# Output bias added on GpSimd while the rows are copied; one DMA per expert for the pad rows; products whose result nothing reads; other banks for the token features

## The chip, the cores and the metric

The kernel runs on one core of a Trainium2 chip. The metric is the device time of one execution in microseconds (us), as the median of several runs. The profile shows one execution of its own: its span goes from the first to the last instruction.

The engines are TensorE (PE; its weight loads are shown as PEld), VectorE (DVE), ScalarE (ACT), GpSimd (POOL) and SyncE (SP), which here issues most DMAs. A q behind a name is that engine's sequencer.

## The reference, cut to what matters

A state space kernel makes 16 x 256 token rows of width 512 from `x`; a class token is put in front. Then come a gated linear recurrence over time with an output product and a skip product, and a mixture of experts (8 experts, 2 for each token, and a shared one):

```python
h = _L0_tok_ref(x, log_dt, B_ri, inv_A_real, A_imag, 512)      # (16, 256, 512)
h = concatenate([broadcast_to(cls_tok, ...), h], axis=1)
...
gates = einsum('btd,de->bte', u, W_in) + b_in      # u: layernorm of layernorm(h)
h_t = (1.0 - a_t) * h_{t-1} + a_t * b_t;  y_t = h_t * tanh(c_t)
out = einsum('bts,sd->btd', y, W_out) + b_out
out = out + einsum('btd,de->bte', x, W_skip) + b_skip
h = h + out
...
h = h + routed(layernorm(h)) + shared(layernorm(h))
```

The change touches where `b_out + b_skip` is added.

## The kernel before, in words

**First stage (lines 293 to 551).** Weights are loaded by SP in 13 jobs, cut into a high and a low f16 half by ScalarE (`st_hi`) and VectorE (`low_half`). VectorE builds tables of powers of the state space poles. At its end it makes `brow` (lines 545 to 547), the sum of the two output biases as two f16 halves in partitions 0 and 32; `ones_row` is a stationary operand of ones.

**Token rounds (`body(k, q)` of every engine, k = -1 to 17; NCH = 16, LAST = 17).** `iterate` (line 705) unrolls k = -1 to 3, loops over ten, and unrolls the rest. A tile number n holds 16 time steps of 16 sequences, 256 rows in two tiles of 128; n = 0 is the class token alone. What this document calls round k is `body(k)`. In it TensorE does, in this order:

- `gate_up_shared(0..3)` of tile k - 1 (line 1018; all its products are L997 of the helper `split3`), with banks `BH` = 1, 2, 0 in turn, then `ranks` (L1043 to L1047);
- `project(0)` of tile k (line 1049): the skip product (L997 with 512 columns) into bank `BS`, the output product (L1059 to L1061) and the bias product `ones_row` x `brow` (L1062) into `BY`;
- `gate_up_shared(4, 5)`, `project(1)`, and `shared_down(0, 1)` (L1072 to L1076) into banks `BD` = 3, 0;
- `input_project` of tile k + 1 (L997), `features` for the tokens of tile k + 2 (line 1001, 64 f32 products, L1011, into `BU` = banks 1 and 2), and the router's products (L997 with 8 columns).

ScalarE copies the features out of `BU` (`tok_out`, L1202), and `gate_up_shared(0)` of the next round waits for that. SP stores them to `h_tok` (L876) and loads them back as rows `hx` in the next round (L819). VectorE takes their statistics (`stats2`, L1521), GpSimd the power -1/2 (L927, L928), ScalarE normalizes (`normalized`, L1222 and L1227) and later copies `hx` to `hc` (L1272), so that `hx` can be loaded again (`c_prom`). VectorE evicts `project` into `h2` (`project_out`: L1540 adds `hc` to the skip product, L1541 adds the output product), evicts `shared_down` (`down_out`, L1553), and makes the operands of `features` (`tok_p`: L1351, L1356; `tok_e`: L1331, L1338, L1339). Nearly all of VectorE's instructions wait for the one before (`link`). GpSimd also scatters the normalized rows to the experts' slots in DRAM, `x_slots` (L941), and computes inv3 and off3 (L950, L951).

In each round SP also loads one unit of expert weights (`load_unit`); ScalarE and VectorE cut it into halves, and SP stores it to `w_halves` (`store_unit`). The first eight units are brought to `wexp` by one DMA that ScalarE issues (line 1300), the other eight by SP during the expert stage, one at every second slot (line 897).

**Pad rows.** Between the experts' rows in `x_slots` unused rows must hold zeros and a row number to which their result is added. `pad_rows(eng, e)` (line 775), called in round NCH by SP for e = 0 to 5 and by ScalarE for 6 and 7, issues two DMAs per expert: 384 pieces of 64 bytes from `pads` (L779) and 384 of 2048 bytes of zeros from `zrow` (L781). Four of SP's six stand ahead of the transposes of `x3w` into `x3T` (L858), which the router's products wait for.

**Expert stage.** 71 slots of 128 rows: TensorE does `gate_up` (L1146, L1147) and, two slots behind, `down` (L1156); the results are added to `out` by an indirect DMA of GpSimd (L975).

The order of work on each engine is the order of its `body`; there is no planner.

## Time and profile before

| | us |
|---|---|
| runs | 1201.67, 1191.70, 1199.46 |
| median | 1199.46 |
| profiled execution, its own time | 1196.48 |
| its span | 1194.8 |
| PE busy | 1059.5 |
| DVE busy | 812.2 |
| POOL busy | 383.9 |
| ACT busy | 347.2 |

The mean granted TensorE clock is 0.944 of full speed. Busy time adds up the instructions; matmuls are pipelined, so that PE's busy time says little of how near it is to its peak. The first stage takes the first 60 us, the token rounds last until about 773 us, and the expert stage takes the rest.

### The profile page before, as it was taken

How to read it: one execution, taken by the hardware profiler on the slowest of the kernel's cores; microseconds unless marked ns; L12 is line 12 of the kernel's file. 1: busy time of each engine (PE TensorE's matmuls, PEld its weight loads, DVE VectorE, ACT ScalarE, POOL GpSimd, SP SyncE). 2: the span in 40 equal slices, each digit the busy share in tenths (PEclk: the TensorE clock that was granted, in tenths of full speed). 3: DMA queues.
4: the chain of work that ended last, by engine and by line, in shares of the span. 5: the costliest groups of instructions: out<-in, count | busy, mean ns of one | idle time of the engine just before them, and what ended most of it. 6: DMA issues, size and time to landing. Idle time of an engine off the chain costs nothing.

```text
span 1194.8 us, 26490 instructions
## 1 busy us (share of the span) xinstructions
PE 1059.5 (89%) x7869; PEld 696.9 (58%) x7870; DVE 812.2 (68%) x2123; ACT 347.2 (29%) x658; POOL 383.9 (32%) x352
## 2 busy tenths in 40 slices
PE   3046898999999999999999994989999999999995
PEld 3034566666766676667766771655555555555552
DVE  7976988898889888988898563544444444444442
ACT  4413433443344333443344332111111111111110
POOL 1011221222123211332022210145545656655554
PEclk8556998999999999999999997899999999999998
DMA  7322456455545555455535589689998777877885
GB/s 247 112 53 54 105 159 154 124 152 173 149 127 150 170 151 143 139 171 162 165 112 157 170 258 371 188 170 217 224 172 132 130 130 130 134 132 128 133 124 74
DMA packets 311150, 183.57 MB, mean 154 GB/s; under 512 B 261218, under 2 KB 280034, under 8 KB 309044
## 3 DMA queue, kind: packets, MB, share of 16 engines
q1 hardware_dynamic: 292948, 135.83, 46.8%
q0 software_dynamic: 15504, 36.46, 15.2%
q10 hardware_dynamic: 2640, 10.54, 2.3%
q8 instruction: 32, 0.52, 0.2%
q14 instruction: 26, 0.21, 0.1%
HBM read 53.40 MB, written 79.73 MB: 111 GB/s over the span
## 4 chain that ended last, share of the span: by engine, by line
PE 75%; DVE 3%; SPq 3%; DMA 3%; issue 2%; ACT 1%; POOLq 0%; POOL 0%; ACTq 0%; DVEq 0%
PE bank L997 30%; PE bank L1146 10%; PE bank L1156 10%; PE bank L1147 10%; PE bank L1072 8%; PE bank L1011 4%; DMA out<-x2w,rows_in 2%; SPq L779 1%; SPq L781 1%; PE bank L1076 1%; ACT tokens L1202 1%; PE bank L1062 1%; DMA wexp<-w_halves 1%; PE bank L1075 1%; DVE wexp L1351 0%
## 5 line engine op out<-in xcount | busy, mean ns | idle before, releaser
L997 PE MATMUL bank<-wexp 128*128 128x256 f16 (+2 forms) x3252 | 418.6, 291 | 24.8 <-issue 9.5
L997 PEld LDWEIGHTS bank<-wexp 128*128 128x128 f16 x3252 | 316.4, 101 | 110.7 <-issue 33.7
L1146 PE MATMUL bank<-wexp,rows_in 128*128 x852 | 255.5, 313 | 9.6 <-issue 6.9
L1147 PE MATMUL bank<-wexp,rows_in 128*128 x852 | 255.1, 312 | 0.0
L975 POOL DMA_INDIRECT out<-x2w,rows_in x71 | 113.7, 1601 | 116.0 <-DMA out<-x2w,rows_in 82.8
L927 POOL TENSOR_TENSOR inv<-var,power 128x4 f32<-128x4 f32 x17 | 29.2, 1717 | 375.0 <-DVE var L1533 375.0
L1689 DVE SCALAR_TENSOR_TENSOR mixed<-bank,mixed 128x352 f32<-128x352 f32 x71 | 37.2, 525 | 161.0 <-ACT mixed L1308 108.4
L963 POOL TENSOR_TENSOR ex<-base,ld 128x8 f32<-128x8 f32 x71 | 120.7, 1699 | 75.9 <-DVE ld L1668 56.0
L1146 PEld LDWEIGHTS bank<-wexp,rows_in 128*128 128x128 f16 x852 | 83.1, 98 | 66.6 <-issue 25.9
L1308 ACT ACTIVATE mixed<-bank 128x352 f32<-128x352 f32 x71 | 32.9, 464 | 295.3 <-PE bank L1147 295.3
L1156 PE MATMUL bank<-wexp,gates 128*128 (+1 forms) x477 | 111.7, 379 | 2.9 <-DVE x2w L1684 2.9
L1072 PE MATMUL bank<-wexp 128*128 128x512 f16 x495 | 112.6, 380 | 0.0
L1147 PEld LDWEIGHTS bank<-wexp,rows_in 128*128 128x128 f16 x852 | 83.2, 98 | 44.2
L1011 PE MATMUL bank<-wexp 64*128 64x64 f32 x1024 | 63.9, 283 | 46.8 <-DVE wexp L1356 46.8
L941 POOL DMA_INDIRECT x_slots<-x3w,sl x66 | 69.8, 1057 | 85.1 <-DVE sl L1413 67.9
L1209 ACT ACTIVATE sgs<-bank 128x256 f32<-128x256 f32 (+1 forms) x102 | 38.4, 376 | 199.5 <-PE bank L997 197.6
L1011 PEld LDWEIGHTS bank<-wexp 64*128 64x128 f32 x1024 | 61.7, 197 | 50.4 <-issue 49.3
L1072 PEld LDWEIGHTS bank<-wexp 128*128 128x128 f16 x495 | 45.8, 98 | 57.9 <-issue 7.2
L1351 DVE TENSOR_TENSOR wexp<-wexp 128x1024 f32 (+1 forms) x64 | 77.8, 1221 | 0.8 <-issue 0.2
L1156 PEld LDWEIGHTS bank<-wexp,gates 128*128 128x128 f16 (+1 forms) x477 | 46.6, 98 | 53.0 <-issue 4.2
L1374 DVE SCALAR_TENSOR_TENSOR gf<-bank,sgs 128x256 f32<-128x256 f32 (+1 forms) x102 | 42.5, 416 | 45.6 <-ACT sgs L1209 38.7
L1691 DVE TENSOR_TENSOR mixed<-mixed 128x352 f16<-128x352 f32 x71 | 37.3, 525 | 41.8 <-ACT mixed L1312 40.1
(281 smaller groups left out, 1247.3 us busy)
## 6 DMA issues: line engine op xcount, KB each, us to landing
w_halves<-rows_in SPq DMA_DIRECT2D x16, 704.0 KB
wexp<-w_halves ACTq DMA_DIRECT2D x1, 8704.0 KB
wexp<-w_halves SPq DMA_DIRECT2D x8, 1088.0 KB
h_tok<-tokens SPq DMA_DIRECT2D x16, 512.0 KB, 2.7
mixed<-h_tok SPq DMA_DIRECT2D x32, 256.0 KB
out<-h SPq DMA_DIRECT2D x32, 256.0 KB
w_halves<-rows_in SPq DMA_DIRECT2D x16, 384.0 KB
rows_in<-in_L_ffn_w_gate SPq DMA_DIRECT2D x16, 352.0 KB, 5.4
```

The source lines that it names most:

```text
L941: nc.gpsimd.indirect_dma_start(out=xs_d.bitcast(I32), out_offset=bass.IndirectOffsetOnAxis(ap=sl[:, i, c:c + 1], axis=0), in_=x3w[:, i, :] ...
L963: nc.gpsimd.tensor_tensor(ex[:, b % 2, 0, :], base[:], ld[:, b % 2, :], ALU.pow).then_inc(d_ex, 1)
L975: nc.gpsimd.indirect_dma_start(out=out_rows, out_offset=bass.IndirectOffsetOnAxis(ap=ext[b][:, E:E + 1].bitcast(I32), axis=0), in_=yo[b % ...
L997: last = MM(dst, stat_of(step, a), mov_of(step, b), start=(s_ == 0 and a + b == 0), stop=(s_ == len(steps) - 1 and a == 1))
L1011: last = MM(BU[t][:, j * NA:(j + 1) * NA], pp[q, f, j].rearrange("p b c -> p (b c)"), ea[q, f, j, :], start=(f == 0), stop=(f == 1))
L1072: MM(BD[i][:], gT[:, m, a, t], wsd[:, m, b, :], start=(m == 0 and a + b == 0), stop=False)
L1146: MM(GB[:, 0:H], xT[b][:, a, c, :], wexp[:, u, o:o + H], start=s_, stop=e_)
L1147: last = MM(UB[:, 0:H], xT[b][:, a, c, :], wexp[:, u, o + H:o + 2 * H], start=s_, stop=e_)
L1156: last = MM(DB[:], gT2[b % 4][0:HK[c], a, c, :], wexp[0:HK[c], bass.ds(unit, 2), o:o + D // 2], start=(c == 0 and a + w == 0), stop=(c == ...
L1209: A(sgs[P - p1:P, m % 2, 0:w], BH[m % 3][0:p1, 0:w], ACT.Silu, scale=SXW).then_inc(c_sg, 1)
L1351: ch.do(TT((pp, pt)[f % 2][:, f // 2], cc, hh, ALU.mult))
L1374: STT(gf[p0:P, m % 2, 0:w], u, SXW, sgs[p0:P, m % 2, 0:w], ALU.mult, ALU.mult).then_inc(c_gm, 1)
```

## The change

1. **Bias.** `bias` [128, 512] f32 and `bsk` are loaded with both biases broadcast to all partitions and added on VectorE at the end of the first stage; `brow`, `ones_row` and L1062 go (33 products). The copy of `hx` to `hc` goes from ScalarE to GpSimd, at the end of its `body`, as an addition of `bias`.
2. **Pad rows.** `pads` in DRAM holds whole rows of 2112 bytes. Its zeros are written in round 1 by four DMAs of SP, its numbers in round 2. `pad_rows` is one DMA. SP's call for e = 4 stands between the two transposes of `x3w`.
3. **Banks.** `BU` = `BD` (banks 3 and 0). `features` waits for `c_dev` in place of `c_gm`; the wait for `c_toke` stands at m = 2 of `gate_up_shared` in place of m = 0.
4. **Products whose result nothing reads.** 36 before `features` of round -1, 10 after a wait for `c_toke` and 28 ahead of `input_project` in round 0, all into `BD[0]`.
5. **Expert weights.** The DMA of line 1300 stands at the head of ScalarE's `body(15)` in place of its end. The other eight units are loaded at every third slot from slot 1, and SP's part of the expert stage is unrolled for 24 slots in place of 16.

```diff
-                sp.dma_start(bo[:, 0, :], b_out.rearrange("(a n) -> a n", a=1)).then_inc(p_in, 16)
-                sp.dma_start(bo[:, 1, :], b_skip.rearrange("(a n) -> a n", a=1)).then_inc(p_in, 16)
+                sp.dma_start(bias[:], b_out.rearrange("(a n) -> a n", a=1).broadcast_to([P, D])).then_inc(p_in, 16)
+                sp.dma_start(bsk[:], b_skip.rearrange("(a n) -> a n", a=1).broadcast_to([P, D])).then_inc(p_in, 16)
...
-                ch.do(nc.vector.memset(brow[:], 0.0))
...
-                link(TT(bo[:, 2, :], bo[:, 0, :], bo[:, 1, :], ALU.add))
-                link(TS(brow[0:1, :], bo[:, 2, :], SW * SY, None, ALU.mult))
-                link(STT(brow[32:33, :], bo[:, 2, :], SW * SY, brow[0:1, :], ALU.mult, ALU.subtract))
+                link(TT(bias[:], bias[:], bsk[:], ALU.add))
...
-        BU = [psum[1], psum[2]]
         BH = [psum[1], psum[2], psum[0]]
         BD = [psum[3], psum[0]]
+        BU = BD
...
-            eng.dma_start(xs_d[bass.ds(row, 3 * P), 2 * D:XW].bitcast(I32),
-                          pads_d[e].rearrange("r q w -> (r q) w")[bass.ds(turn, 3 * P)]).then_inc(c_z, 16)
-            eng.dma_start(xs_d[bass.ds(row, 3 * P), 0:2 * D].bitcast(I32).rearrange("(i p) w -> p i w", p=P),
-                          zrow[:, 0:2 * D].bitcast(I32).rearrange("p (o w) -> p o w", o=1).broadcast_to([P, 3, D])).then_inc(c_z, 16)
+            eng.dma_start(xs_d[bass.ds(row, 3 * P), :], pads_d[e].rearrange("r q w -> (r q) w")[bass.ds(turn, 3 * P), :]).then_inc(c_z, 16)
...
                         for i in range(tiles(n)):
+                            if i == 1 and isinstance(k, int) and k == NCH:
+                                pad_rows(sp, 4)
                             sp.wait_ge(c_lo3, n * 2 + (i + 1) * 2 // tiles(n))
...
                     if isinstance(k, int) and k == NCH:
-                        for e in range(4, 6):
-                            pad_rows(sp, e)
+                        pad_rows(sp, 5)
...
+                    if isinstance(k, int) and k == 1:
+                        for r in range(4):
+                            sp.dma_start(pads_d[:, r, :, 0:2 * D].bitcast(I32).rearrange("e q w -> q e w"),
+                                         zrow[:, 0:2 * D].bitcast(I32).rearrange("p (o w) -> p o w", o=1).broadcast_to([P, E, D])).then_inc(c_pw, 16)
...
-                    if isinstance(i, int) and i < 2 * E and i % 2:
-                        u = E + i // 2
+                    if isinstance(i, int) and i < 3 * E and i % 3 == 1:
+                        u = E + i // 3
                         sp.dma_start(wexp[:, u, :], w16_d[u]).then_inc(d_w, 16)
...
+                    if has(k + 1):
+                        n, nt = k + 1, tiles(k + 1)
+                        gp.wait_ge(c_hx, (n + 1) * 32)
+                        at_least(gp, c_oev, n * 2)
+                        apart(gp, c_sep)
+                        TT(hc[:, 0:nt, :], hx[:, 0:nt, :], bias[:].rearrange("p (o d) -> p o d", o=1).broadcast_to([P, nt, D]),
+                           ALU.add).then_inc(c_prom, 1)
...
                     if not isinstance(k, int) or k >= 1:
-                        pe.wait_ge(c_gm, k * 6)
+                        pe.wait_ge(c_dev, k * 2)
...
+                        if m == 2:
                             at_least(pe, c_toke, clampc(k + 1) * 2)
-                        if m == 2:
                             at_least(pe, c_dev, n * 2)
...
-                        MM(BY[:], yT[:, 1, t], wout[:, 0, :], start=False, stop=False)
-                        MM(BY[:], ones_row[:], brow[:], start=False, stop=True).then_inc(c_out, 2 // tiles(n))
+                        MM(BY[:], yT[:, 1, t], wout[:, 0, :], start=False, stop=True).then_inc(c_out, 2 // tiles(n))
...
+                    def idle_products(count):
+
+                        for i in range(count):
+                            MM(BD[0][:], ident16[:], wskip[:, 0, 0, :], start=True, stop=True)
+
                     if isinstance(k, int) and k == -1:
+                        idle_products(36)
                         features(k)
+                    if isinstance(k, int) and k == 0:
+                        pe.wait_ge(c_toke, 2)
+                        idle_products(10)
...
+                    if isinstance(k, int) and k == 0:
+                        idle_products(28)
                     if first_win:
                         input_project()
...
                 def body(k, q):
+                    if isinstance(k, int) and k == NCH - 1:
+
+
+                        act.wait_ge(c_tokm, NCH * 2)
+                        act.wait_ge(c_wo, 32 * E)
+                        act.dma_start(wexp[:, 0:E, :], w16_d[0:E].rearrange("u p n -> p u n")).then_inc(d_w, 16)
...
-                    if has(k + 1):
-                        n, nt = k + 1, tiles(k + 1)
-                        at_least(act, c_oev, n * 2)
-                        A(hc[:, 0:nt, :], hx[:, 0:nt, :], ACT.Copy).then_inc(c_prom, 1)
```

The waits on `c_pw`, `c_z` and `p_gp` follow the new counts.

## Rows read from the trace of the kernel before

**Rows 1.** The page's chain that ended last, shares of the span by engine

```profile
PE 75%; DVE 3%; SPq 3%; DMA 3%; issue 2%; ACT 1%; POOLq 0%; POOL 0%; ACTq 0%; DVEq 0%
```

**Rows 2.** Windows, two rounds: length, busy us per engine, PEclk, DMA share, GB/s

```profile
391.01:431.32 40.31, 39.75 (x327) 27.73 (x328) 34.38 (x79) 15.17 (x29) 9.01 (x11) 0.96 0.49 146
431.32:470.01 38.69, 38.13 (x328) 26.91 (x328) 34.34 (x79) 15.28 (x29) 8.98 (x11) 1.00 0.51 152
```

**Rows 3.** PE timeline, round from 431.32: start, length, line, operation [idle before <-releaser]

```profile
452.55 0.38 PE L1061 MATMUL bank<-wexp,yT 128*128 128x512 f16 x1
453.18 3.41 PE L1072 MATMUL bank<-wexp 128*128 128x512 f16 x15
464.97 3.79 PE L1011 MATMUL bank<-wexp 64*128 64x64 f32 x64
470.01 5.19 PE L997 MATMUL bank<-wexp 128*128 128x256 f16 x46 [0.56 <-ACT tokens L1202]
```

**Rows 4.** DVE timeline of the same round

```profile
437.19 0.42 DVE L1374 SCALAR_TENSOR_TENSOR gf<-bank,sgs 128x256 f32<-128x256 f32 x1 [1.21 <-ACT sgs L1209]
439.91 0.42 DVE L1374 SCALAR_TENSOR_TENSOR gf<-bank,sgs 128x256 f32<-128x256 f32 x1 [0.22 <-ACT sgs L1209]
462.11 0.68 DVE L1553 SCALAR_TENSOR_TENSOR h<-bank,h 128x512 f32<-128x512 f32 x1
468.83 0.69 DVE L1338 TENSOR_TENSOR wexp<-wexp 128x512 f32<-128x512 f32 x1 [0.89 <-PE bank L1011]
```

**Rows 5.** POOL timeline: first stage, round -1, and the round from 431.32

```profile
1.40 0.99 POOL L324 MEMSET zrow<- 128x1056 f16 x1
68.38 1.24 POOL L928 TENSOR_TENSOR off<-neg,inv 128x2 f32<-128x2 f32 x1 [0.18 <-POOL inv L927]
458.04 0.60 POOL L951 TENSOR_TENSOR off<-neg,inv 128x1 f32<-128x1 f32 x1 [0.18 <-POOL inv L950]
```

**Rows 6.** Line L1351, all its instructions: ns min/median/max, first and last start

```profile
L1351 DVE TENSOR_TENSOR wexp<-wexp x64: 1215/1219/1227, 66.1 to 650.7; 128x1024 f32 x40, 128x1024 f32<-128x1024 f32 x24
```

**Rows 7.** DVE timeline, end of the first stage

```profile
52.72 0.68 DVE L545 TENSOR_TENSOR bo<-bo 1x512 f32<-1x512 f32 x1
```

**Rows 8.** PE timeline, rounds -1 and 0

```profile
73.25 7.09 PE L1011 MATMUL bank<-wexp 64*128 64x64 f32 x64 [46.15 <-DVE wexp L1356]
103.50 6.10 PE L997 MATMUL bank<-wexp 128*128 128x256 f16 x36 [8.75 <-issue]
```

**Rows 9.** SP and DVE timelines, rounds 1 and 2

```profile
148.10 0.38 SPq L876 DMA_DIRECT2D h_tok<-tokens  x1
158.84 1.28 DVE L1521 BATCH_NORM_STATS2 stat<-mixed 128x6 f32<-128x512 f32 x2
```

**Rows 10.** DMA issues of the first 30 us: queue, KB, us to landing

```profile
x_slots<-zrow SPq DMA_DIRECT2D x1, 1792.0 KB, 13.4
x_slots<-zt SPq DMA_DIRECT2D x1, 56.0 KB, 12.8
```

**Rows 11.** Window in round 16: the same columns as rows 2

```profile
718.00:722.00 4.00, 4.00 (x19) 1.62 (x18) 1.78 (x4) 1.14 (x3) 0.00 (x0) 1.00 1.02 424
```

**Rows 12.** ACT, SP and PE timelines, round 16

```profile
699.19 0.44 ACTq L1300 DMA_DIRECT2D wexp<-w_halves  x1
717.73 8.72 SPq L779 DMA_DIRECT2D x_slots<-pads  x1
748.47 0.48 PE L997 MATMUL bank<-gw,wexp 128*128 128x8 f16 x12 [19.27 <-DMA wexp<-x3w]
```

**Rows 13.** DMA issues: all 16 of one form, then its one after 700 us

```profile
rows_in<-in_L_ffn_w_down SPq DMA_DIRECT2D x16, 256.0 KB, 4.6
rows_in<-in_L_ffn_w_down SPq DMA_DIRECT2D x1, 256.0 KB, 28.6
```

**Rows 14.** Windows in the expert stage: the same columns as rows 2

```profile
829.00:884.00 55.00, 51.30 (x301) 29.02 (x300) 23.47 (x81) 8.64 (x18) 28.75 (x18) 1.00 1.19 211
884.00:928.00 44.00, 43.81 (x260) 25.22 (x259) 20.60 (x72) 7.68 (x16) 26.10 (x16) 1.00 0.80 132
```

More of the change, by code:

```diff
@@ L210, in vit_tower @@
             bin_ = t0("bin_", [P, 3], F32)
-            bo = t0("bo", [1, 3, D], F32)
+            bsk = t0("bsk", [P, D], F32)
             st = [t0(f"st{i}", [P, 4, D], F32) for i in range(2)]
@@ L324, in _ @@
                 nc.gpsimd.memset(zrow[:], 0.0).then_inc(p_gp, 1)
-                nc.gpsimd.memset(ones_row[:], 1.0).then_inc(p_gp, 1)
-                gp.wait_ge(p_gp, 6)
+                gp.wait_ge(p_gp, 5)
                 for m in (ident16, identf):
@@ L381, in _ @@
             def _(pe):
-                pe.wait_ge(p_gp, 8)
+                pe.wait_ge(p_gp, 7)
                 def turn(g):
@@ L828, in body @@
                         sp.wait_ge(c_ri, 1)
-                        sp.wait_ge(c_pw, 64)
+                        sp.wait_ge(c_pw, 128)
                         for e in range(4):
@@ L900, in _ @@
                 sp.wait_ge(d_w, 16)
-                over_tiles(sp, serve, 2)
+                over_tiles(sp, serve, 3)
                 for b in range(2):
@@ L936, in body @@
                         if isinstance(k, int) and k == LAST:
[L937 removed]
+                            gp.wait_ge(c_z, 16 * E)
                         apart(gp, c_sep)
@@ L1254, in body @@
                         act.wait_ge(c_ri, 1)
-                        act.wait_ge(c_pw, 64)
+                        act.wait_ge(c_pw, 128)
                         pad_rows(act, 6)
@@ L1294, in body @@
                         gate_tanh()
-                    if isinstance(k, int) and k == NCH - 1:
-                        act.wait_ge(c_tokm, NCH * 2)
-                        act.wait_ge(c_wo, 32 * E)
-                        act.dma_start(wexp[:, 0:E, :], w16_d[0:E].rearrange("u p n -> p u n")).then_inc(d_w, 16)
                 act.wait_ge(c_cst, 2)
```

14 lines of the change are left out of this document (6 added, 8 removed).

## The prediction

> **What bounds the kernel now.** I read the chain that ended last first: TensorE has 75% of it, no other engine over 3% [rows 1]. So a product taken away counts where TensorE is not waiting, and a wait counts where TensorE is what waits. Then I cut the span into rounds by the start of L997 after the router's products. From round 3 to 14 a round takes 38.7 us, or 40.3 us where the granted clock dipped (mean 0.96 in place of 1.00): four of these twelve rounds have that dip, at 1.62 us each [rows 2]. TensorE is busy 98% of such a round, with one hole, the 0.56 us at the start where L997 waits for ScalarE's copy of the token features [rows 3]. VectorE is busy 34.4 of the 38.7 us [rows 2], and its instructions are linked one to the next, so that its real idle time in the round is only 1.21 + 0.22 + 0.89 = 2.3 us, in three waits [rows 4]. That is the second bound, and the one to keep in mind: a round cannot go under about 36.4 us for VectorE, whatever TensorE saves.
>
> **Rounds 3 to 14, TensorE's side.** Between the start of the third L1061-type product and the first product of L1072 lie 0.63 us, the deleted L1062 in between; 15 products of L1072 have a pace of (3.41 - 0.38) / 14 = 0.22 us [rows 3]. Without L1062 the gap is one pace: 0.41 us saved, twice a round, 0.82 us. The new banks move the wait for the features' copy to the third group (m = 2), over 5 us later, when the copy is long done: the 0.56 us go too. TensorE's round becomes 38.69 - 1.38 = 37.31 us. The price of the banks is a new wait of `features` for both `down_out`s: the second starts at 462.11 and takes 0.68 us, `features` starts at 464.97 [rows 3, 4]. Of 2.2 us slack, 0.8 go with the products, so it still costs nothing while VectorE keeps its times. Queued behind it are the router's products and the whole next round.
>
> **The same rounds, the copy of the rows.** ScalarE loses a copy it had time for (busy 15.3 of 38.7 us [rows 2]): nothing. GpSimd gets an addition of 128x1024 f32 with two SBUF inputs after its last L951, from about 458.8 [rows 5]. No row has such an operation. From below: VectorE does that shape in 1.22 us [rows 6]. From above: a memset of 1056 columns took GpSimd 0.99 us [rows 5]; two reads and a write at that pace are 2.9 us. Its own lateness costs nothing, since SP asks for it in the next round, ten us on. What may cost is the way to SBUF: L928 on two columns took 1.24 us at 68.38 while VectorE ran four L1351 back to back, against 0.2 to 0.3 elsewhere [rows 5], so GpSimd waits until a VectorE instruction of two SBUF inputs is over. The reverse is not seen: 64 L1351 took 1.215 to 1.227 us, beside GpSimd's short operations or not [rows 6]. A long one may hold VectorE's L1356, which is due at 459.24, by 0 to 2.6 us. I take 1.3 us, near the lower end because the only rows are those in which VectorE is not held. What VectorE can do, 36.4 us a round, then becomes 36.4 + 1.3 = 37.7 us, more than TensorE's 37.31: `features` waits 0.4 us for the second `down_out`, and the round is VectorE's. The gain is 1.0 us a round, 12 rounds: **-12 us**. Without any hold it is 12 x 1.38 = -16.5.
>
> The Trainium skill speaks against this edit: "SBUF — State Buffer", section "Who interferes with whom", says that VectorE with two SBUF inputs and GpSimd reading SBUF exclude each other, the first to issue keeping the shared ports for its whole instruction. By "GPSIMD Engine Reference", section 3.1, an addition of 2048 elements takes 4.5 us there, so some 2.3 us as an estimate here. The 1.24 us of L928 agree with the rule for one direction; the other direction no row shows.
>
> **First stage and first rounds.** At the end of the first stage VectorE is last: three operations (0.68 [rows 7], 0.42, 0.68) give way to one of 0.68. The biases now arrive as 256 KB each in place of 2 KB, and the first activation waits for all nine small loads: I give back 0.7 us. **-0.5 us**. The 36 idle products run while TensorE waits 46 us for VectorE. `features(-1)` took 7.09 us with the clock at its lower level (1.2 GHz), 3.79 us in a round at 1.00, which is 2.4 GHz [rows 3, 8]: 3.3 us, all on the path, since ScalarE's copy, the store and the load of the next rows follow it. The 10 and the 28 cover the wait for yT and the 8.75 us before L997 at 103.50, whose 36 products took 6.10 us [rows 8] and need 4.1 at the 5.19 us for 46 of rows 3; they are ended before their data come. Perhaps 2.2 us of the other cold products return. **-5.5 us**.
>
> **The zero rows in round 1.** Four new DMAs on SP write 4 x 2 MB = 8.4 MB in 2 KB pieces right behind the store at 148.10 [rows 9]. Behind them on the same queue stand the rows hx of tile 3, the weight unit's loads and stores, and the transposes. Is a queue served in order? The 56 KB of zt, issued 1.3 us behind 1792 KB of zeros, landed after 12.8 us [rows 10]: yes. The most that the engines moved is 424 GB/s [rows 11]; 8.4 MB are 20 us. So hx lands at about 148.5 + 1.5 + 20 + 3.5 = 173.5 in the times of before; `stats2` takes it at 158.84 [rows 9]. Behind `stats2` on VectorE stand `project_out` and all else, and rounds 1 and 2 are the ones that VectorE bounds: **+14.5 us**. Add GpSimd's hold in those two rounds, **+2.6 us**.
>
> **The load of wexp one round earlier.** ScalarE issued it at 699.19 [rows 12]; at the head of the body it comes at about 663.6. Before, it filled the DMA engines from 702 to 746 us and the pad rows had to be issued through them: one issue alone held SP for 8.72 us, and x3T came so late that TensorE stood 19.27 us [rows 12]. With the load gone from there, one DMA of whole rows for two per expert, and only pad row 4 between the transposes, I expect x3T of tile 1 12.5 us after its `project`, as in other rounds, plus 2 us of pad traffic: a hole of some 6.5 us, 13 gained. But round 15 now meets the load. The small loads issued beside it landed after 28.6 us, where 4.6 is the median of their 16 [rows 13]: two queues get turns by packets, not by bytes. hx of tile 16 is 2048 packets of 256 B, 128 for each engine; the load is 64 packets of 8.7 KB for each. It will land with the end of the load, some 27 us into the round, where `stats2` wants it at 10.5; TensorE has 4 us slack there: +12.2. Together **-0.8 us**. In rounds 15 and 16, where VectorE has little to do, the products give 2 x 0.82 + 0.56 = **-2.2 us**.
>
> **Expert stage.** Between 829 and 884 us TensorE lost 3.7 of 55 us with the DMA share at 1.19; with no loads of weight units left the share was 0.80 and the loss 0.2 of 44 [rows 14]. Every third slot in place of every second thins the loads by a third, over a longer stretch. Of some 5 us lost to them in all, **-3 us**.
>
> **Sum.** -12 - 0.5 - 5.5 + 14.5 + 2.6 - 0.8 - 2.2 - 3 = -6.9. From the profiled execution (1196.5 us; its span is 1194.8) that is 1189.6, say **1190 us**; the median of the three runs, 1199.5, lies 3 us above the profiled one, which is inside their spread of 10 us.
>
> **Rivals.** *GpSimd's addition holds VectorE fully* (0.25). By the port rule above it starts while VectorE is in `down_out`, gets the ports, and holds L1356 to its end: 2.0 to 2.6 us. Then VectorE's `down_out` is what `features` waits for, and the round is 38.4 to 39.0 us. The point from which it decides is a hold of 0.9 us; from 2.3 us on a round is longer than the 38.69 of before. At 2.6: +3.7 in place of -12, and 2.6 more in rounds 1 and 2: **1208 us**, slower. For it: L928. Against: 64 unchanged L1351. *The zero rows are hidden* (0.25): the engines serve hx beside them, or hx is early enough: without 14.5, **1175 us**; with hx of tile 16 on time as well, 1163. For it: DMA stands idle half of rounds 1 and 2. Against: the order that zt shows. *The clock decides, not the products* (0.10): the stretch of `features` and the router is where the clock fell in 4 of 12 rounds; a change of where the waits lie can give it to all twelve (+13, **1203 us**) or to none (-6.5, 1183). Then the change doesn't do what it says in those rounds.
>
> **Chances.** The forecast has 0.40, with a range of its own of 1182 to 1199. For eight in ten I reach down to 1168 and up to 1209. About 1% can be told from no change here. Faster by more (below 1187.5): the hidden rows, a third of the forecast, half of the clock's case: 0.44. Slower by more (above 1211.5): 0.15. Within: 0.41.
>
> **What would show it.** In the profile after: rounds of 37.3 to 38 us from 3 to 14 with no ScalarE wait at their start; if a hold, L1356 late or longer beside a GpSimd addition of 2 us, and `features` waiting for L1553. In round 2 a wait of `stats2` for hx of about 14 us, and one of some 16 us in round 15; a hole under 8 us in place of 19.27. If both waits for hx are missing I am wrong by 25 us. If the addition takes over 4 us, the round is VectorE's or GpSimd's and the sum falls on the other side.

## The result: slower by 1.4%, and the profile after

The changed kernel took 1212.0 us (median of four runs, 1210.4 to 1214.0) where the kernel before, run beside it, took 1195.6 (1191.2 to 1201.7): a ratio of 1.0138, 95% interval 1.010 to 1.018. Forecast were 1190 us and a range of 1168 to 1209. The profiled execution took 1213.5 us (span 1211.8), 17.0 us over that of before.

The page's chain that ended last, after, against [rows 1]:

```profile
PE 39%; DVE 29%; issue 10%; DMA 6%; SPq 2%; ACT 1%; DVEq 1%; POOL 0%; POOLq 0%; ACTq 0%
```

VectorE has 29% of the chain where it had 3%: the rounds changed hands. To see where the 17 us are I cut both spans at one instruction: the second eviction of `shared_down` in each round (L1553 before, L1562 after; round 1 has one).

| stretch | before | after | difference | forecast |
|---|---|---|---|---|
| first stage | 60.3 | 62.6 | +2.3 | -0.5 |
| to the end of round 1 | 79.8 | 79.6 | -0.1 | -4.2 |
| rounds 2 and 3 | 84.8 | 110.2 | +25.4 | +14.8 |
| rounds 4 to 14 | 430.5 | 421.1 | -9.4 | -11.0 |
| rounds 15 to 17 | 118.1 | 118.5 | +0.4 | -3.0 |
| expert stage | 421.2 | 419.7 | -1.6 | -3.0 |

The first stage is taken to end at VectorE's first instruction of the rounds (L1654 before, L1663 after). The last column is my sum, spread over the same stretches (the 2.6 us of hold half to round 1, half to round 2). Its 23.9 us of error have no one place.

**A steady round.** Windows of two rounds after; columns as in [rows 2]:

```profile
442.90:480.79 37.89, 37.19 (x327) 26.84 (x325) 35.76 (x80) 14.22 (x28) 11.30 (x12) 1.00 0.53 156
480.79:518.98 38.19, 37.38 (x327) 26.92 (x325) 35.78 (x80) 14.22 (x28) 11.45 (x12) 1.00 0.52 154
```

VectorE is busy 35.8 us where it was 34.3 [rows 2]. The 1.4 us more are in one instruction. Timelines of VectorE, GpSimd and TensorE around the end of a round after, and the line L1365 (L1356 before) as a whole:

```profile
475.71 0.69 DVE L1562 SCALAR_TENSOR_TENSOR h<-bank,h 128x512 f32<-128x512 f32 x1
476.32 3.94 DVE L1365 TENSOR_TENSOR wexp<-wexp 128x1024 f32<-128x1024 f32 x2
480.19 0.68 DVE L1486 SCALAR_TENSOR_TENSOR x3w<-wexp,x3w 128x512 f16<-128x512 f32 x1
480.79 0.68 DVE L1562 SCALAR_TENSOR_TENSOR h<-bank,h 128x512 f32<-128x512 f32 x1
```

```profile
475.68 2.37 POOL L954 TENSOR_TENSOR mixed<-mixed,bias 128x1024 f32<-128x1024 f32 x1
```

```profile
443.73 3.79 PE L1015 MATMUL bank<-wexp 64*128 64x64 f32 x64 [0.70 <-DVE h L1562]
```

```profile
L1365 DVE TENSOR_TENSOR wexp<-wexp x32: 1209/1221/2810, 73.0 to 671.9; 128x1024 f32<-128x1024 f32 x32
```

GpSimd starts its addition 0.03 us ahead of a VectorE instruction that reads PSUM and one SBUF operand, and that one keeps its 0.69 us. The next, with two SBUF operands, starts at 476.32 and takes 2.8 us in place of 1.2: it ends 1.1 us after GpSimd does (478.05), which is about its own length. Two of them took 3.94 us, where they took 2.35 before. So the hold is 1.5 to 1.6 us, and `features` waits 0.70 us for the second `down_out`. By the Trainium skill ("SBUF — State Buffer", section "Who interferes with whom") the first to issue keeps the shared ports for its whole instruction; this is the direction that no row of before showed, and the trace agrees.

**First stage and first rounds.** ScalarE's first activation, which VectorE's chain waits for, and TensorE's timeline in rounds -1 and 1:

```profile
9.67 0.20 ACT L347 ACTIVATE pw_<-dtj 128x2 f32<-128x2 f32 x1 [7.55 <-DMA bsk<-in_L_attn_b_skip]
```

```profile
63.24 9.35 PE L1085 MATMUL bank<-wexp,ident 128*128 128x512 f16 x36 [34.43 <-DVE m L1666]
76.38 7.09 PE L1015 MATMUL bank<-wexp 64*128 64x64 f32 x64 [3.79 <-DVE wexp L1365]
...
146.78 5.97 PE L1015 MATMUL bank<-wexp 64*128 64x64 f32 x64 [2.52 <-DVE wexp L1365]
```

Windows of round -1 after, columns as in [rows 2]:

```profile
66.13:76.37 10.24, 6.46 (x30) 2.74 (x28) 9.95 (x15) 1.44 (x2) 5.29 (x3) 1.00 0.01 2
76.37:86.61 10.24, 10.23 (x95) 10.12 (x96) 4.49 (x9) 1.09 (x2) 0.00 (x0) 0.50 0.25 73
```

Before, that activation started at 6.23 us: the two broadcast loads make it 3.4 us late, of which 2.3 are left at the end of the stage. The 36 idle products ended 3.8 us ahead of `features(-1)`, which took 7.09 us, exactly as in [rows 8]. They did raise the granted clock, to 1.00 from 66.1 us on; it fell back to 0.50 at 76.37, just as `features(-1)` started after those 3.8 idle us. In round 1 `features` had waited 0.7 us and run at 2.4 GHz before; now it waits 2.5 us and takes 5.97 in place of 3.79.

**Rounds 2, 15 and 16.** SP's queue behind the store of round 1, then VectorE in round 2:

```profile
153.96 0.38 SPq L869 DMA_DIRECT2D h_tok<-tokens  x1
154.37 12.45 SPq L872 DMA_DIRECT2D pads<-zrow  x4
166.94 10.84 SPq L811 DMA_DIRECT2D mixed<-h_tok  x2
```

```profile
182.44 1.29 DVE L1530 BATCH_NORM_STATS2 stat<-mixed 128x6 f32<-128x512 f32 x2 [17.79 <-DMA mixed<-h_tok]
```

The zeros went at 377 GB/s (window 166 to 170), and `stats2` got its `hx` 28.5 us after the store was issued. In round 15, VectorE, TensorE, and the DMA issues from 666 to 730 us:

```profile
707.76 1.29 DVE L1530 BATCH_NORM_STATS2 stat<-mixed 128x6 f32<-128x512 f32 x2 [17.09 <-DMA mixed<-h_tok]
```

```profile
712.92 5.29 PE L1001 MATMUL bank<-wexp 128*128 128x512 f16 x12 [13.21 <-DVE h L1550]
763.59 0.48 PE L1001 MATMUL bank<-gw,wexp 128*128 128x8 f16 x12 [3.79 <-DMA wexp<-x3w]
766.73 0.48 PE L1001 MATMUL bank<-gw,wexp 128*128 128x8 f16 x12 [2.65 <-DMA wexp<-x3w]
```

```profile
wexp<-w_halves ACTq DMA_DIRECT2D x1, 8704.0 KB, 27.3
...
h_tok<-tokens SPq DMA_DIRECT2D x1, 512.0 KB, 10.4
```

All as forecast: the store beside the load of `wexp` lands after 10.4 us (median of all: 2.7), `stats2` waits 17.1 us, TensorE 13.2, and the hole of 19.27 [rows 12] is 6.4 us in two parts.

### The profile page after: what moved, and what is told of

It reads as the page before. It is cut to its first block, busy times and chain, and to the rows that moved or that the text cites. A ratio compares the mean times of both kernels' runs of the same rounds, so it can differ in the third digit from the quotient of the medians.

```text
span 1211.8 us, 26540 instructions
## 1 busy us (share of the span) xinstructions
PE 1068.8 (88%) x7910; PEld 706.1 (58%) x7911; DVE 834.4 (69%) x2120; ACT 330.2 (27%) x641; POOL 421.4 (35%) x368
## 4 chain that ended last, share of the span: by engine, by line
PE 39%; DVE 29%; issue 10%; DMA 6%; SPq 2%; ACT 1%; DVEq 1%; POOL 0%; POOLq 0%; ACTq 0%
PE bank L1160 10%; PE bank L1170 10%; PE bank L1161 10%; PE bank L1001 5%; DVE wexp L1360 3%; DMA mixed<-h_tok 2%; DVE wexp L1340 2%; DVE wexp L1376 2%; DVE h L1549 2%; DVE h L1550 2%; DVE stat L1552 2%; DVE x3w L1486 2%; DVE wexp L1365 1%; DVE stat L1530 1%; PE bank L1015 1%
## 5 line engine op out<-in xcount | busy, mean ns | idle before, releaser
L1001 PE MATMUL bank<-wexp 128*128 128x256 f16 (+2 forms) x3252 | 419.5, 291 | 42.9 <-DVE h L1550 31.7
L1001 PEld LDWEIGHTS bank<-wexp 128*128 128x128 f16 x3252 | 316.3, 101 | 130.7 <-DVE h L1550 32.4
L1170 PE MATMUL bank<-wexp,gates 128*128 (+1 forms) x477 | 111.7, 379 | 2.6 <-DVE x2w L1693 2.6
L1015 PE MATMUL bank<-wexp 64*128 64x64 f32 x1024 | 67.8, 293 | 16.2 <-DVE h L1562 9.7
L1360 DVE TENSOR_TENSOR wexp<-wexp 128x1024 f32 (+1 forms) x64 | 77.8, 1221 | 1.4 <-issue 1.0
L1015 PEld LDWEIGHTS bank<-wexp 64*128 64x128 f32 x1024 | 65.8, 207 | 20.4 <-issue 13.3
```

The costliest lines, as they stand in the source:

```text
L1001: last = MM(dst, stat_of(step, a), mov_of(step, b), start=(s_ == 0 and a + b == 0), stop=(s_ == len(steps) - 1 and a == 1))
L1015: last = MM(BU[t][:, j * NA:(j + 1) * NA], pp[q, f, j].rearrange("p b c -> p (b c)"), ea[q, f, j, :], start=(f == 0), stop=(f == 1))
L1170: last = MM(DB[:], gT2[b % 4][0:HK[c], a, c, :], wexp[0:HK[c], bass.ds(unit, 2), o:o + D // 2], start=(c == 0 and a + w == 0), stop=(c == ...
L1360: ch.do(TT((pp, pt)[f % 2][:, f // 2], cc, hh, ALU.mult))
```

## The experiments

Each ran beside the kernel before. First the stretches of the table above, in us, from the one profile that each kernel has (rounds 4 to 14 hold up to three dips of the clock, 0.6 to 2.9 us each, and in e7 and e9 one of 4.2):

| kernel | first stage | to end of 1 | 2, 3 | 4 to 14 | 15 to 17 | expert | ratio to before |
|---|---|---|---|---|---|---|---|
| changed | 62.6 | 79.6 | 110.2 | 421.1 | 118.5 | 419.7 | 1.0138 |
| e1 zeros in the first stage | 65.3 | 77.9 | 93.8 | 421.5 | 117.7 | 419.7 | 1.0062 |
| e2 bias on TensorE | 60.5 | 76.2 | 103.2 | 419.0 | 122.7 | 420.4 | 1.0034 |
| e3 addition in the gap | 63.8 | 77.8 | 106.2 | 409.9 | 119.8 | 420.2 | 1.0036 |
| e4 load at the end | 63.7 | 79.7 | 111.4 | 423.8 | 118.3 | 419.2 | 1.0128 |
| e5 before, bias alone | 63.8 | 79.3 | 93.0 | 420.4 | 112.7 | 418.8 | 0.9982 |
| e6 load in mid-round | 64.6 | 79.4 | 108.9 | 423.7 | 118.6 | 419.7 | 1.0197 |
| e7 zeros spread | 63.3 | 79.8 | 91.6 | 423.0 | 119.1 | 418.7 | 1.0037 |
| e8 no idle products | 63.9 | 78.1 | 111.3 | 423.7 | 118.7 | 418.8 | 1.0173 |
| e9 pads undone | 63.4 | 79.8 | 91.6 | 428.5 | 116.5 | 424.2 | 1.0040 |
| e10 load in pieces | 63.4 | 79.6 | 110.2 | 424.7 | 114.7 | 419.5 | 1.0167 |
| e11 four repairs | 59.4 | 75.9 | 88.5 | 409.9 | 123.6 | 417.9 | 0.9824 |
| e12 the same, bias on TensorE | 60.5 | 76.2 | 85.6 | 418.9 | 113.6 | 418.1 | 0.9879 |
| e13 e5 with products | 63.4 | 80.5 | 88.9 | 419.5 | 114.1 | 417.9 | 0.9922 |
| e14 pieces on SP | 63.6 | 78.2 | 111.2 | 421.3 | 111.7 | 419.7 | 1.0103 |
| e15 e11, pieces on SP | 59.1 | 76.7 | 89.0 | 411.7 | 111.1 | 422.5 | 0.9762 |
| e16 e15 with products | 59.5 | 76.2 | 88.0 | 409.9 | 108.2 | 423.1 | 0.9741 |

The intervals of the ratios are 0.0025 to 0.008 wide to each side; those that matter stand in the text. A stretch of a single profile has a scatter of its own: with the load of `wexp` at the same place, rounds 15 to 17 take 116.5 to 122.7 us (changed, e1, e2, e3, e7, e8, e9).

The dips are not spread evenly. Where TensorE has no wait next to `features` in a steady round (e2, e3, e11, e12, e15, e16), rounds 4 to 14 hold one dip in six profiles; where it waits 0.5 to 0.7 us there (before and all others), every profile has one to three. A whole stretch of e3, rounds 4 to 14, columns as in [rows 2]:

```profile
247.80:657.70 409.90, 409.25 (x3578) 295.23 (x3575) 383.60 (x860) 157.43 (x308) 126.07 (x132) 1.00 0.54 159
```

That the wait brings the dips is how I read it; no run adds the wait alone.

### The zeros (e1, e7, e9)

e1 and e7 move the same four DMAs, e9 undoes part 2 (no zeros in `pads`, `pad_rows` as two DMAs):

In e1 they stand behind the weight loads 6, 8 and 12 of the first stage, in e7 behind `load_unit` of rounds 0 to 2 and ahead of the transposes:

```diff
-                    if isinstance(k, int) and k == 1:
-                        for r in range(4):
...
+                    for r in {6: (0, 1), 8: (2,), 12: (3,)}.get(i, ()):
...
```

```diff
+                    if isinstance(k, int) and 0 <= k < 3:
+                        for r in ((0, 1), (2,), (3,))[k]:
...
```

> The changed kernel with one thing moved: the four DMAs that write the zeros of the pad rows (8.4 MB) are issued by SP in the first stage, between its weight loads, in place of round 1. Theory (a queue is served in order, so the rows hx stood behind the zeros): the wait of stats2 for hx in round 2 (17.8 us) goes, rounds 2 and 3 take what they took before, and the time falls by 19 to 24 us, from 1212 to 1188 to 1193. Rival 1 (the zeros cost as much wherever they are, through the DMA engines): the weight loads of the first stage are late in turn, the first stage ends 5 us or more later than its 63, and the time falls by 12 or less. Rival 2 (something else than hx is late in round 2): it falls by under 5.

Measured: 1201.7 us, 10 less than the changed kernel, not 19 to 24. The wait of `stats2` is gone and rounds 2 and 3 fall by 16.4 us to 93.8, but not to the 84.8 of before; the first stage takes 65.3. So rival 1 holds in part (the first stage is 2.7 us longer, not 5), and 9 us of rounds 2 and 3 are not the zeros'.

> The changed kernel with the four DMAs of zeros issued where SP's queue has nothing due for ten us: two in round 0, one each in rounds 1 and 2, each behind the loads of hx and of the weight unit and ahead of the transposes of x2w. Theory (only the order on the queue costs): round 2 falls from 67.0 us to 49, as with the zeros in the first stage, and the first stage keeps its 62.6 to 63.7 us (with the zeros in it: 65.3): 1190 to 1195. Rival (8.4 MB delay whatever moves beside them in the DMA engines too): the transposes of rounds 0 to 2 are late, each round 2 to 5 us longer, 1200 to 1205.

Measured: 1199.1 us (ratio 1.0003 to 1.0071), 4 over the range expected, rounds 2 and 3 at 91.6, round 2 at 47.5, the first stage at 63.3. Rounds 2 and 3 fall by 18.6 us, the median of the runs by 12.9; the profile has 1.9 us of the difference in rounds 4 to 14, in a longer dip, and the ten runs spread over 14 us. 8.4 MB moved beside rounds 0 to 2 cost nothing that can be seen where the queue had time; in rounds 2 and 3 the order on the queue was the whole cost, 18.6 us.

> The changed kernel with part 2 (the pad rows) undone: no zeros written in round 1, two DMAs for each expert in round 16 as before, in the order of before. Theory: round 2 is 49 to 50 us in place of 67.0 (as in the run with the bias alone, 49.6), the first stage stays at 62.6 to 63.8 us; rounds 15 to 17 are 118 us as in the changed kernel, since what costs there is the load of wexp: 1194 to 1198, 17 us under the changed kernel. Rival (the single DMA for each expert gains something in round 16, as its 13 us shorter hole suggests): rounds 15 to 17 take 123 to 130 us, 1200 to 1207.

Measured: 1201.2 us. Rounds 2 and 3 take 91.6 as with the zeros spread, though here no zeros are written at all: a second witness. Rounds 15 to 17 take 116.5, so the two DMAs for each expert were no loss there. The total is 3 us over the range expected: in the profile the expert stage took 424.2, for a reason that I did not find, and rounds 4 to 14 took 428.5 with three dips.

### The bias (e2, e3, e5, e13)

e2 undoes part 1 in the changed kernel. e3 keeps it and moves two things: GpSimd's addition (`add_bias`) goes ahead of its second power of the round, and VectorE's first `down_out` ahead of `rows_lo(k, 0)` and the fourth `tok_p`:

```diff
                         for i in range(nt):
+                            if i == nt - 1 and has(k + 1):
+                                add_bias(k + 1)
                             gp.wait_ge(c_st3, n * 2 + (i + 1) * 2 // nt)
...
+                    if shared:
+                        down_out(0)
...
```

> The changed kernel with part 1 (the bias) undone: the bias product on TensorE again, the copy of hx to hc on ScalarE, the small loads of before; all else as changed. Theory (GpSimd's addition holds VectorE for 1.5 us of every round and so takes back what TensorE saves): rounds 3 to 14 become TensorE's again at 38.69 - 0.56 = 38.1 us, with the dips of the clock visible in some, +0 to +6 over 12 rounds; the first stage gives back 2.3 and the first rounds some 2 to 3. Together 1207 to 1213: part 1 as made is worth about nothing. Rival (the addition costs nothing that matters, and the slower time is all from the zero rows and the load of wexp): 12 x 0.82 = 10 us more in the rounds against 2 less in the first stage, 1218 to 1222.

Measured: 1202.1 us, better than expected: ratio 1.0034 against 1.0138. Rounds 4 to 14 take 419.0, as with part 1 (421.1 with one dip), which is the theory; 38.09 us each, as the 38.13 worked out for TensorE. But the first stage, rounds -1 to 1 and rounds 2 and 3 gave 2.1 + 3.4 + 7.0 us, where I expected 4 to 5. Rounds 15 to 17 took 4.2 of it back. Part 1 as made was a loss of 10 us, and it arises early. `features(-1)` shows one piece of it:

```profile
73.29 5.45 PE L1013 MATMUL bank<-wexp 64*128 64x64 f32 x64 [2.39 <-DVE wexp L1368]
```

Without the addition beside VectorE's last operand of round -1 (2.17 us in the changed kernel, 1.2 here), `features(-1)` starts 2.4 us after the 36 products in place of 3.8, and takes 5.45 us in place of 7.09.

> The changed kernel, all of its work kept, but GpSimd's addition is issued before its second power of the round, where VectorE runs instructions that read PSUM or one SBUF input, and VectorE does its first down_out before rows_lo(0) and the fourth tok_p. Theory (the addition holds a VectorE instruction with two SBUF inputs for as long as it runs): the long L1365 (2.7 us) is 1.22 again, VectorE's floor is 36.4 to 36.9 us, and a round is TensorE's at 37.3 to 37.5 us: 0.6 us less in 12 rounds, less what dips of the clock give back, 1203 to 1208. Rival (L1365 is long for another reason, as its place beside the end of the round's DMAs): L1365 stays at 2.7, rounds stay at 38.0 to 38.2, 1211 to 1213.

Measured: 1200.3 us, 12 less than the changed kernel and under the range. VectorE at the end of a round, GpSimd, and windows of two rounds of e3:

```profile
466.26 1.25 DVE L1491 SCALAR_TENSOR_TENSOR x3w<-wexp,x3w 128x512 f16<-128x512 f32 x1
467.44 1.21 DVE L1365 TENSOR_TENSOR wexp<-wexp 128x1024 f32 x1
468.68 2.36 DVE L1370 TENSOR_TENSOR wexp<-wexp 128x1024 f32<-128x1024 f32 x2
```

```profile
464.61 2.35 POOL L923 TENSOR_TENSOR mixed<-mixed,bias 128x1024 f32<-128x1024 f32 x1 [3.35 <-DVE h L1555]
```

```profile
434.51:471.56 37.05, 37.05 (x327) 26.75 (x325) 34.83 (x79) 14.33 (x28) 11.46 (x12) 1.00 0.54 159
471.56:509.08 37.52, 37.37 (x328) 26.94 (x327) 34.97 (x80) 14.33 (x28) 11.48 (x12) 1.00 0.53 157
```

The pair of L1370 takes 2.36 us again. The hold has moved with the addition and shrunk: L1491, the only instruction with two SBUF operands that the addition's tail still meets, takes 1.25 in place of 0.68. TensorE has next to no wait in the round, which takes 37.26 us on average (37.31 worked out).

> The kernel before with part 1 of the change alone: the two biases broadcast and added, GpSimd's addition at the end of its body, no bias product, no copy on ScalarE. Theory from the run with part 1 undone (which gained 10 us, all of it ahead of round 4): first stage +2 to +3.5 (VectorE's first dependent instruction waits for the two 256 KB loads), rounds -1 to 3 +7 in VectorE's holds and in the clock that TensorE loses while it waits, rounds 4 to 14 -0.5 each with the dips hidden, -8: within 4 us of before, 1196 to 1202. Rival (the early loss in the run with part 1 undone came from its meeting with the zero rows): -5 or better, 1192 or less.

Measured: 1195.2 us, ratio 0.9982 (0.9953 to 1.0011): no difference from before, just under the range. Rounds 4 to 14 give 10 us (38.04 us a round without dips in place of 38.69, and fewer dips), rounds 2 and 3 take 8.2 back, the first stage 3.5 (rounds 15 to 17 gave 5.4, which I did not look into). So the early loss does not need the zeros. Three holds of 1.5 us make 4.5 of the 8.2. What makes the rest? e13 puts ten products ahead of `features` in rounds 1 and 2:

```diff
+                    if isinstance(k, int) and k in (1, 2):
+                        pe.wait_ge(c_gm, k * 6)
+                        for i in range(10):
+                            MM(psum[1][:], ident16[:], wskip[:, 0, 0, :], start=True, stop=True)
                     pe.wait_ge(c_tokp, n)
```

> The kernel before with part 1 alone (1195.2 us, rounds 2 and 3 together 93.0 us where before has 84.9), and ten products whose result nothing reads ahead of features in rounds 1 and 2, where TensorE waited 2.3 to 2.5 us for VectorE and features then took 5.6 to 7.1 us in place of 3.8. Theory (a hold of 1.5 us on VectorE grew to 8 us over two rounds because TensorE, waiting, fell to its lower clock, and its slower products then kept VectorE waiting): features takes 3.8 us in both, and rounds 2 and 3 take 85 to 89 us, 4 to 8 less. Rival (VectorE's own work sets these rounds, whatever TensorE's clock): 92 to 94 us and the same total.

Measured: 1188.8 us, ratio 0.9922 (0.9892 to 0.9953), rounds 2 and 3 at 88.9. TensorE in rounds 1 and 2, and the windows of rounds 2 and 3, first of e5, then of e13:

```profile
147.61 6.47 PE L1014 MATMUL bank<-wexp 64*128 64x64 f32 x64 [2.47 <-DVE wexp L1354]
...
192.16 6.63 PE L1014 MATMUL bank<-wexp 64*128 64x64 f32 x64 [2.32 <-DVE wexp L1354]
```

```profile
143.07:192.64 49.57, 44.09 (x352) 32.45 (x352) 43.39 (x96) 17.17 (x34) 13.35 (x13) 0.90 0.40 115
192.64:236.07 43.43, 41.83 (x333) 30.49 (x332) 37.53 (x84) 13.38 (x26) 11.19 (x12) 0.84 0.54 143
```

```profile
145.76 2.32 PE L1010 MATMUL bank<-wexp,ident 128*128 128x512 f16 x10
148.44 3.79 PE L1018 MATMUL bank<-wexp 64*128 64x64 f32 x64 [0.36 <-DVE wexp L1358]
...
186.35 2.32 PE L1010 MATMUL bank<-wexp,ident 128*128 128x512 f16 x10
189.04 3.79 PE L1018 MATMUL bank<-wexp 64*128 64x64 f32 x64 [0.37 <-DVE wexp L1358]
```

```profile
143.88:189.51 45.63, 44.16 (x372) 30.90 (x372) 43.25 (x95) 17.08 (x34) 13.37 (x13) 1.00 0.43 125
189.51:232.82 43.31, 39.37 (x333) 27.85 (x332) 37.44 (x83) 13.37 (x26) 11.19 (x12) 0.92 0.53 143
```

With the gap filled the clock stays at 1.00 through round 2, `features` takes 3.79 us both times, and round 2 is 3.9 us shorter with VectorE's work unchanged (43.4 and 43.3 us busy). That is the amplifier: a hold of 1.5 us makes TensorE wait 2.3 to 2.5 us, where it had waited 0.7 in round 1 and not at all in round 2; while `features` runs the granted clock is 0.56 and 0.54 on average, and the slower products then keep VectorE waiting. The medians fell by 6.4 us, of which these two rounds are 4.1. Of the 8.2 us of e5, 4.1 were clock and about 4 the holds themselves. The split is rough: the clock is at its lower level for 23.9 us of rounds 2 and 3 in e5, for 6.8 in e13 and for 10.2 in the kernel before.

### The idle products (e8)

> The changed kernel without the 36, 10 and 28 products whose result nothing reads. Theory (the 36 end 3.8 us before features(-1) starts, and by then the granted clock has fallen again; the 10 and the 28 warm the project of round 0, which nobody waits for long): the time changes by less than 2 us, 1210 to 1214. Rival (they do warm what is on the path): 3 to 6 us slower, 1215 to 1218.

Measured: 1214.4 us, ratio 1.0173 (1.010 to 1.025) against 1.0138 (1.010 to 1.018): no difference that can be told. In its profile `features(-1)` took 7.09 us after 48 us of waiting, as with the 36 products; up to round 1 it is not slower, and the rest are dips (rounds 5 and 7). The products of round 0 do warm what follows them: 12 products of `project` take 2.75 us behind them and 5.25 in e8, but nobody waits for these, since `features(0)` starts at 112.96 and 112.67 us. The same kind of product, placed with no gap ahead of `features`, works (e13), and with a gap of 2.4 us in place of 3.8 the 36 work by half (e2).

### The load of wexp (e4, e6, e10, e14)

One place each: the end of `body(15)` (e4), behind `normalized(16)` (e6), eight DMAs on ScalarE's queue from there on (e10), eight on SP's queue (e14, shown):

```diff
                     if htok(k):
                         load_unit(k - 1)
+                    if isinstance(k, int) and k in (NCH - 1, NCH):
...
+                        for u in range(4):
+                            u += 4 * (k - NCH + 1)
+                            sp.dma_start(wexp[:, u, :], w16_d[u]).then_inc(d_w if u == E - 1 else d_w8, 16)
```

> The changed kernel with one thing undone: ScalarE issues the load of wexp (8.7 MB) at the end of its body(15), as before. Theory (the load makes late what is loaded beside it, wherever it stands): the wait of stats2 in round 15 goes, 13 us, and the wait for x3T in round 16 comes back, but not whole, since the pad rows are now one DMA for each expert: a hole of 12 to 19 us in round 16 where it is about 6, in all 1204 to 1212. Rival (the pad rows' two DMAs, not the load, made the hole of before): the hole stays under 8 us, and the time falls by 12 or more, to 1200 or less.

Measured: 1214.8 us. Rounds 15 to 17 take 37.0, 44.8 and 36.4 us in place of 52.9, 33.3 and 32.2: the wait has moved and the sum, 118.3, has not. The hole ahead of the router in round 16 is 22.1 us in two parts (19.27 before), so the single DMA for each expert does not shorten it. The total is a few us over the expected range; that is in rounds 2 to 14, with a second dip.

> The changed kernel, but ScalarE issues the load of wexp in body(15) behind its normalization of tile 16, when the rows hx of tile 16 have landed, in place of ahead of everything. Theory (only what is loaded beside it is late, so place it where nothing stands that is due soon): stats2 in round 15 waits no longer (-13), the transposes of x2w and x3w in rounds 15 and 16 are what runs beside it, and they cost 3 to 8: 1201 to 1207. Rival (the transposes are due as soon as hx was, and wait as long): 1209 to 1214.

Measured: 1217.9 us; rounds 15 to 17 take 37.5, 47.9, 33.2, again 118.6. The wait of `stats2` is gone, and TensorE waits 15.3 us for a transpose of `x2w` instead: the rival, and worse. The three equal sums are in part luck, beside a scatter of 116.5 to 122.7 us with the load at one place.

> The changed kernel, but the load of wexp (8.7 MB) is issued by ScalarE as eight DMAs of one unit each, spread over body(15) from behind the normalization of tile 16 and the start of body(16). So far the sum of rounds 15 to 17 was 118.1 to 118.6 us with the load at the end of body(15), at its head and in its middle. Theory (it is the burst that makes the transposes and rows beside it late, the engines having half of their time free): the sum falls by 6 to 14 us, 1198 to 1206. Rival (the bytes cost their time wherever and however they are issued): the sum stays within 3 us of 118, 1209 to 1215.

Measured: 1216.5 us, over both ranges, with rounds 15 to 17 at 114.7. Less than hoped, and no firm figure, since the same pieces gave 123.6 us in e11 and 113.6 in e12: ScalarE reaches five of its eight points within 13 us, so this is still a burst.

> The changed kernel with the load of wexp in eight DMAs of one unit on SP's own queue, four in round 15 and four in round 16, each time behind the loads of the weight unit and ahead of the transposes. On one queue they cannot stand beside a transpose, only ahead of it. Theory (the transposes of x2w and x3w, of some thousand small packets, are made late by turns with large packets of another queue: 16 us to land where 3.3 is usual): the sum of rounds 15 to 17, 118 us so far and 114.7 with the pieces on ScalarE's queue, falls to 105 to 110: 1199 to 1205. Rival (the bytes are what costs): 115 to 120, 1209 to 1215.

Measured: 1210.1 us, in the rival's range; rounds 15 to 17 at 111.7, 6.8 under the changed kernel, between theory and rival. On one queue it does help: the three profiles with the pieces on SP's queue (e14, e15, e16) take 108.2 to 111.7 us there, the three with them on ScalarE's (e10, e11, e12) 113.6 to 123.6. DMA issues with their time to land, e11 (pieces on ScalarE's queue, see below) from 645 to 690 us and e14 from 670 to 760:

```profile
wexp<-w_halves ACTq DMA_DIRECT2D x5, 1088.0 KB, 11.2
...
wexp<-x2w SPq DMA_TRANSPOSE x2, 16.0
wexp<-x3w SPq DMA_TRANSPOSE x2, 16.6
```

```profile
x_slots<-pads SPq DMA_DIRECT2D x6, 792.0 KB, 14.2
...
wexp<-x3w SPq DMA_TRANSPOSE x5, 4.6
wexp<-x2w SPq DMA_TRANSPOSE x2, 6.6
```

A transpose beside the pieces lands after 16 us, behind them on the same queue after 4.6 to 6.6 (usual: 3.0 to 3.3). That fits what the Trainium skill says ("DMA: Bandwidth & Descriptors", section "Queues, rings and completion order"): an engine goes round the queues that have work for it by packets. What the profile lists as packets are here 256 bytes long for the transposes and 8704 for the pieces. It agrees; it doesn't exclude that the bytes set a floor as well, and what is left of the holes in e14 stands beside the pad rows, which took 14.2 us to land.

### Versions that beat both kernels (e11, e12, e15, e16)

e11 joins e3, e7, e10 and later bias loads (behind the fifth weight load, with a semaphore of their own). e12 has e7 and e10 with the bias on TensorE. e15 is e11 with the load as in e14, and e16 adds the ten products of e13.

> The changed kernel with four repairs: GpSimd's addition in VectorE's gap, the zeros spread over rounds 0 to 2, the two bias loads issued between the weight loads with a semaphore of their own, the load of wexp in eight pieces. If the terms add up (-12, -13, -2, and -10 if the pieces do what they should): 1212 - 37 = 1175, without the gain of the pieces 1185. If the early rounds keep VectorE as their bound and the terms overlap: 1185 to 1190.

Measured: 1173.8 us, ratio 0.9824 (0.9785 to 0.9862), where the terms add up to 1175, but not by them: rounds 15 to 17 took 123.6 us by the transposes above in place of giving 10, and the first stage (59.4, with the bias loads late) and the rounds up to 1 gave 6.9.

> The changed kernel with the bias back on TensorE (part 1 undone), the zeros spread and the load in pieces: from the run with part 1 undone (1202) -13 for the zeros and -10 for the pieces if they work: 1179, without them 1189. Against the version with GpSimd's addition in the gap it tells what the bias on GpSimd is worth once it no longer holds VectorE: the rounds 4 to 14 are 37.2 us there and 38.1 here, 10 us for that one, if the early rounds cost both the same.

Measured: 1180.5 us (median of five runs; a sixth took 1196.2), ratio 0.9879 (0.9837 to 0.9920). Rounds 4 to 14: 409.9 in e11, 418.9 here; rounds 2 and 3: 88.5 and 85.6. So in these rounds the bias on GpSimd is worth 6 us once it is in VectorE's gap (9.0 late, less 2.9 early). The medians, 6.7 us apart, agree, but the two intervals overlap, and in the two profiles rounds 15 to 17 differ by 10.0 us the other way.

> The version that beat both kernels (1173.8 us) with the pieces on SP's queue as in the run before. There rounds 15 to 17 took 123.6 us, since the transposes landed after 16 us. Theory: 105 to 110 us, so 1156 to 1162. Rival (bytes): 118 to 124, 1168 to 1176.

Measured: 1171.8 us, ratio 0.9762 (0.9720 to 0.9803). Rounds 15 to 17 at 111.1, 12.5 less than e11; but one dip, and an expert stage of 422.5 that I can't explain, take most of it back, and the total lies in the range of the rival.

> The same with the ten products ahead of features in rounds 1 and 2. Rounds 2 and 3 together took 88.5 us in the version that beat both. If the clock is what is lost there: 84 to 86, 3 us less than the run before. If GpSimd's addition in the gap leaves TensorE no long wait there, no change within 1 us.

Measured: 1167.5 us, ratio 0.9741 (0.9705 to 0.9777), the best of all, 44 us under the changed kernel. Rounds 2 and 3 gained 1.0 us, not 3; the rest of the 4 us to e15 lies in rounds where nothing was changed. The ten products are worth little once the hold is short.

## Why the prediction was wrong, step by step

- **Rounds 3 to 14, TensorE's side** (37.31 us): right. It can be read where VectorE doesn't hold it: 37.26 in e3. That the banks alone leave 38.13: 38.09 in e2.
- **The copy of the rows** (addition 2.0 to 2.6 us, hold 1.3, period 37.7): the mechanism was right, the addition took 2.36 us, the hold 1.5 to 1.6, the period 38.06. The 1.3 was the middle of 0 to 2.6, not worked out, so that its closeness is luck, and so is the gain over rounds 4 to 14: of the 9.4 us, near the 11, 6.9 are the period and 2.5 the dips, for which the sum had no term. The periods before hold 4.9 us of dips (430.5 less 11 x 38.69), those after 2.4, in one dip. Part 1 gave nothing in these rounds on top of the banks (e2: 38.09 without it); alone it gives the same 38.04 (e5). The two do not add up: with part 1 in, VectorE and the hold set the round, with the banks or without.
- **"Add GpSimd's hold in those two rounds, +2.6 us"**: this step failed. Part 1 alone costs 8.2 us in rounds 2 and 3 (e5). I priced the hold on VectorE as if TensorE's products kept their length, and only as large as 1.3 us. In a stretch where VectorE is the bound and TensorE waits, the wait costs clock: 4.1 us of the 8.2 (e13). The rest is the holds themselves: three of 1.5 us fall in this stretch, and I had added 1.3 us for it. The rival in which the clock decides looked at rounds 3 to 14, where TensorE hardly waits.
- **The zero rows in round 1** (+14.5): the mechanism was right, the size was not. Spread, they free 18.6 us. At 377 GB/s the 8.4 MB are 22.3 us, not 20 at the 424 of [rows 11]; and TensorE comes back at 1.2 GHz: L1001 at 190.03, after 16.3 us of waiting, took 5.3 us where 2.75 is usual at 2.4 GHz.
- **The idle products** (-5.5): this step failed, and it is the second largest miss. I took the clock of `features(-1)` to rise because TensorE was busy for 9 us before. But `features(-1)` starts 13 us after the first stage [rows 8], and 36 products last 8 us at the 0.22 of [rows 3] (9.4 measured): they ended 3.8 us ahead of it, and it ran at 1.2 GHz all the same. The trace of before had both numbers. Part 1 made the gap wider: without it the gap is 2.4 us and 1.6 of the 3.3 us come (e2).
- **"I give back 0.7 us"** for the 256 KB bias loads: mis-sized. It was 3.4 us at the first activation, 2.3 at the end of the stage. Issued later under their own semaphore they cost nothing (59.4 in e11).
- **The load of wexp** (-0.8 as a gain of 13 and a loss of 12.2): both sides came as worked out, a gain of 13 in rounds 16 and 17 and a loss of 13 in round 15. That it gains nothing at any place was not seen: 118.3, 118.5 and 118.6 us at the end, the head and the middle. **Products of rounds 15 and 16** (-2.2): probably hidden in those waits, which no run shows.
- **Expert stage** (-3): -1.6, inside a scatter of 418 to 424 us between kernels with the same loads and instructions there, which stays open; part 5 there was not run alone.
- **The chances**: the forecast's own range of 1182 to 1199 left no room for four small misses on one side. Of the rivals, the full hold of VectorE, 1208 us, was nearest in time and wrong in cause: the steady rounds did not get longer.

## What to carry to other kernels

Before an operation goes from a busy engine to an idle one, look at which SBUF operands the neighbour reads in that moment; the same 2.4 us of GpSimd cost 1.5 us beside a two-operand VectorE instruction and 0.6 when placed mostly beside instructions that read PSUM. The zeros cost by what stood behind them on their queue, and nothing by their bytes once they stood where nothing was due; the load of `wexp` cost by the small-packet transfers beside it on the other queue. So put a large DMA where its queue has nothing due, and look at what runs beside it. And where TensorE waits, price the wait twice, in time and in clock.

## What the runs showed of the hardware

- A wait of 2.3 to 2.5 us ahead of 64 small products made them take 6.0 to 6.6 us in place of 3.79 (changed, e5); with ten filler products in the gap (wait 0.4 us) they took 3.79 (e13). In round -1, 36 filler products raised the granted clock to 1.00; when they ended 3.8 us early the 64 ran at 0.50 (7.09 us), at 2.4 us early they took 5.45 (e2).
- Rounds 4 to 14 of the six profiles in which TensorE has no wait next to `features` hold one dip of the granted clock; the twelve with a wait of 0.5 to 0.7 us there hold one to three each.
- GpSimd's addition of 128x1024 f32 with two SBUF inputs takes 2.35 us. The one of 128x512, half as much, took 2.23 in round -1, where a VectorE instruction with two SBUF operands was under way as it started; that GpSimd was held there fits, but no run shows its free length.
- With two 256 KB loads broadcast from one row, the first instruction that waits for them started 3.4 us later than with two of 2 KB at the same place of the queue.
- None of the three places of one 8.7 MB load shortened the sum over three rounds (118.3 to 118.6 us; kernels with it at one place spread over 6 us).
